# A two-layer adaLN network on one core: gates fixed with channels on partitions, the last pieces of layer 0 moved into the first attention steps, and one residual sum moved ahead

## Chip, cores and metric

The kernel runs on one core of one Trainium2 chip. The metric is the device time of one execution in microseconds (us), lower is better; the median of the runs counts. A profiled execution also gives a span (first to last instruction) and a time of its own.

## What is computed

Eight inputs (B = 8) of 512 rows by 128 channels pass through two adaLN layers. The reference, cut to what matters:

```python
mod = (silu(L0_c) @ L0_wmod)            # per input: sa, ca, ga, sb, cb, gb, 128 channels each
ga = (2 * (ga >= 0) - 1) * maximum(abs(ga), 0.25)      # the same for gb, and in layer 1
x = x + ga * rwkv_attention(layernorm(x) * (1 + ca) + sa)     # a scan over the 512 rows
x = x + gb * (fp6_quantised(layernorm(x) * (1 + cb) + sb) @ wd.T + bias)
# layer 1, with its own mod
h = layernorm(x) * (1 + ca) + sa
gate = softmax((h @ w_gate).mean(rows)) # 3 numbers per input
idx = sort(top_k(h @ w_imp, 32))        # 32 selected rows per input
out = gate0 * attn(q, latent keys) + gate1 * attn(q, selected keys) + gate2 * attn(q, window keys)
x = x + ga * (out @ w_proj)             # 16 heads of 96 channels, 32 value channels
h = layernorm(x) * (1 + cb) + sb
x = x + gb * tanh(h @ wo.T + c_final @ uo.T + bo)   # c_final: a cell that runs over the 8 inputs
```

## The kernel before

Everything stays in SBUF. The program is written out by hand for five engines, each with its own stream; semaphores join them. It has three parts.

**Setup.** TensorE makes all modulation columns in one PSUM bank (L1609); VectorE copies them to `modc` (L1151: channels on partitions, 12 kinds by 8 inputs). Four kinds are needed as rows as well (the same 128 values on all partitions), because they scale the columns of `woT` and of the dequantised weight or the rows of the second norm. For each input TensorE makes these four with a 128x512 product (L1616) and layer 1's output gates with a 128x128 product (L1617); ScalarE copies the first to `modrow` (`row_read`, L816), VectorE the second to `garow1` (`row_reads`, L1162). VectorE then fixes the gates (sign, at least 0.25; `gate_fix`, L1124 to L1129) on 128x1024 elements three times: for `modrow[:, :, 0]`, for `modrow[:, :, 3]` and later for `garow1`. `ffn_rows` (L1172, L1173) adds one to the scales and makes the bias row.

**Start: layer 0.** A loop over `b` from -2 to 9 is written out, a round per value. In round `b` the engines work at different inputs: moments of input `b+2` (`norm_mix`, VectorE), key maxima of `b+1` (`maxima`, L1202 and L1206), the scan `wkv` of `b` (L1212 to L1232), first residual sum of `b` with its moments (`norm_ffn`, L1237), quantisation of `b-1` (`quantised_ffn`, L1077 to L1089), second residual sum of `b-1` with its moments (`norm_attention`, L1247), and layer 1's norm and transposition into `HT` of `b-2`. VectorE's order within a round is: `wkv(b)`, `quantised_ffn(b-1)`, `maxima(b+1)`, `norm_ffn(b)`, `keep_moments(b-2)`, `norm_mix(b+2)`, `norm_attention(b-1)`. GpSimd turns moments into scale and shift (`deviation`), modulates (L656, L658), decodes the codes (`decode`, L651), rotates queries and keys (`rope`, L663 to L676). ScalarE normalises (L820) and makes the exponentials (L848 to L854) that `wkv` of the next round waits for. The first projections for layer 1's attention go through one shared PSUM bank, bank 7, in the order of the table `SLOTS`: TensorE fills it (`fill`), ScalarE or VectorE reads it (`read`), and the next fill waits for that read. The scores of rows (`score`, L1679) are summed in bank 5 in two halves of four inputs; the top 32 of the first half are found in round 6. After round 9 TensorE makes the gate logits (`gate_logits`, L1859).

**Attention: layer 1.** 32 groups of four heads, four groups per input. A group has 24 units (a unit is the score tiles of one head); `RU` = 12 units of the latent keys, then 12 of the window keys. `FIRST` is the first group, `FULL` a loop of four groups, seven times, and `LAST` the rest. `group_tasks` says at which unit which fill of bank 7 stands. SyncE moves rotated and projected parts into place by DMA (`lay_group`: 4 KB runs, four DMAs a part); TensorE waits for all of a group's parts in front of its unit 0. In `FIRST` VectorE also finds the top 32 of the second half of the inputs (units 0 to 12) and the softmax of the gates.

## Time and profile before

| | before |
|---|---|
| median of 3 runs | 2014.3 us (2013.28 to 2017.04) |
| the profiled execution's own time | 2014.44 us |
| its span | 2012.6 us |
| TensorE busy | 1822.4 us, 91% |
| VectorE busy | 1287.3 us, 64% |
| ScalarE busy | 1173.0 us, 58% |
| GpSimd busy | 677.5 us, 34% |
| mean granted TensorE clock | 0.947 |

Busy shares are averages over parts that differ: in the first seventh of the span VectorE is the busiest, behind it TensorE. They say where to look; what a part is worth is read from its timeline. In the timeline, a number in square brackets is the idle time of that engine just before the instruction, and the name behind the arrow is what ended it.

### The profile page before, as it was taken

The page shows a single profiled execution, that of the slowest core. Times are in us where ns is not written, and L with a number is a line of the kernel's source. Part 1 is how long each engine was busy: PE and PEld are TensorE (multiplying, and loading weights), DVE is VectorE, ACT ScalarE, POOL GpSimd, SP SyncE. Part 2 cuts the span into 40 slices and gives each one's busy share as a digit, 9 for nine tenths or more (in the row PEclk, how much of TensorE's full clock was granted, in tenths as well). Part 3 has the DMA queues.
Part 4 walks back from the last instruction along what each step waited for, and adds up shares of the span by engine and source line. Part 5 has one row for each costly group of instructions (what it writes and reads, how often), then busy time and mean ns, then how long its engine had stood idle before and what let it go on. Part 6 is the DMA issues. An engine that isn't in the chain of part 4 may idle for free.

```text
span 2012.6 us, 38380 instructions
## 1 busy us (share of the span) xinstructions
PE 1822.4 (91%) x10672; PEld 1076.1 (53%) x10672; DVE 1287.3 (64%) x3817; ACT 1173.0 (58%) x3572; POOL 677.5 (34%) x698
## 2 busy tenths in 40 slices
PE   5575789999999999999999999999999999999996
PEld 3332445555555555655555555555655556555552
DVE  6999666656566666666666656665666666666672
ACT  3464356656565656666565656665666566666651
POOL 1456433343233323333343333332333234333300
PEclk8778589999999999999999999999999999999998
DMA  4001021111011111121112111120111111211101
GB/s 157 1 0 27 15 58 38 38 43 52 24 40 39 47 35 38 42 48 48 39 38 52 48 26 47 35 54 20 44 43 38 49 38 38 52 48 38 37 1 42
DMA packets 71346, 81.42 MB, mean 40 GB/s; under 512 B 29521, under 2 KB 37842, under 8 KB 70994
## 3 DMA queue, kind: packets, MB, share of 16 engines
q1 hardware_dynamic: 71122, 78.74, 15.4%
q8 instruction: 103, 1.69, 0.4%
q14 instruction: 121, 0.99, 0.2%
HBM read 7.90 MB, written 2.10 MB: 5 GB/s over the span
## 4 chain that ended last, share of the span: by engine, by line
issue 49%; PE 21%; POOL 19%; DVE 8%; ACT 2%; POOLq 1%; DMA 0%; DVEq 0%; SPq 0%; ACTq 0%
PE bank L1822 6%; PE bank L1849 3%; POOL arena L674 3%; PE bank L1783 3%; POOL arena L676 3%; POOL arena L663 2%; POOL arena L673 2%; POOL arena L664 2%; PE bank L1688 2%; POOL arena L672 1%; POOL arena L712 1%; DVE arena L1225 1%; PE bank L1683 1%; PE bank L1746 1%; PE bank L1729 1%
## 5 line engine op out<-in xcount | busy, mean ns | idle before, releaser
L1425 DVE CUSTOM_DVE_ANT_0 arena<-bank,W 128x512 f32<-128x512 f32 (+3 forms) x1024 | 480.6, 488 | 523.0 <-PE bank L1822 363.9
L980 ACT ACTIVATE arena<-arena 128x512 f32<-128x512 f32 (+3 forms) x1024 | 570.4, 560 | 369.5 <-DVE arena L1425 366.6
L1822 PE MATMUL bank<-arena 96*128 96x512 f32 (+6 forms) x2048 | 716.5, 452 | 15.9 <-issue 14.5
L1822 PEld LDWEIGHTS bank<-arena 96*128 96x128 f32 x2048 | 350.2, 192 | 190.5 <-issue 154.5
L1849 PE MATMUL bank<-W,arena 128*128 128x128 f32 x2560 | 430.0, 282 | 0.1
L1849 PEld LDWEIGHTS bank<-W,arena 128*128 128x128 f32 x2560 | 301.4, 144 | 222.1 <-issue 183.3
L1436 DVE COPY arena<-bank 128x512 f32<-128x512 f32 (+1 forms) x512 | 318.5, 622 | 78.6 <-PE bank L1849 75.8
L712 POOL TENSOR_TENSOR arena<-arena,one 128x512 f32<-128x512 f32 x64 | 66.8, 1044 | 812.2 <-DVE arena L1393 806.2
L1783 PE MATMUL bank<-arena 128*32 128x256 f32 (+1 forms) x3072 | 223.2, 363 | 1.9 <-DVE arena L1436 1.8
L980 ACT ACTIVATION_READ_ACCUMULATOR arena<-arena 128x1 f32 x1024 | 197.3, 193 | 0.0
L959 ACT ACTIVATE arena<-bank 128x384 f32<-128x384 f32 x256 | 124.6, 487 | 94.4 <-PE bank L1849 92.6
L1783 PEld LDWEIGHTS bank<-arena 128*32 128x32 f32 x3072 | 61.0, 108 | 184.8 <-issue 158.9
L663 POOL TENSOR_TENSOR arena<-arena,W 128x512 f32<-128x512 f32 x64 | 69.9, 1092 | 205.4 <-ACT arena L898 205.4
L974 ACT ACTIVATE arena<-bank 128x32 f32<-128x32 f32 (+1 forms) x384 | 65.2, 205 | 105.0 <-DVE arena L1425 103.8
L1688 PE MATMUL bank<-arena,W 128*128 128x512 f32 x192 | 103.1, 619 | 21.9 <-ACT arena L898 21.8
L1687 PE MATMUL bank<-arena,LW 96*128 96x512 f32 x192 | 103.3, 620 | 2.8 <-ACT arena L898 2.7
L672 POOL TENSOR_TENSOR arena<-arena 128x512 f32<-128x512 f32 x64 | 81.4, 1272 | 56.1 <-DMA arena<-arena 50.0
L1623 PE MATMUL bank<-W,arena 128*128 128x128 f32 x160 | 34.0, 351 | 71.6 <-ACT arena L820 45.3
L898 ACT ACTIVATE arena<-bank 128x512 f32<-128x512 f32 x128 | 76.2, 595 | 33.4 <-PE bank L1687 19.4
L1425 DVE DVE_READ_ACCUMULATOR2_ANT arena<- 128x1 f32 x1024 | 84.8, 83 | 0.0
L676 POOL TENSOR_TENSOR arena<-arena 128x512 f32<-128x512 f32 x64 | 81.3, 1270 | 5.0
L674 POOL TENSOR_TENSOR arena<-arena,W 128x512 f32<-128x512 f32 x64 | 78.0, 1220 | 0.0
(265 smaller groups left out, 2221.0 us busy)
## 6 DMA issues: line engine op xcount, KB each, us to landing
arena<-arena SPq DMA_DIRECT2D x896, 64.0 KB, 2.0
arena<-arena SPq DMA_DIRECT2D x64, 128.0 KB, 2.6
W<-wide SPq DMA_DIRECT2D x1, 3730.0 KB, 13.4
X<-x SPq DMA_DIRECT2D x8, 256.0 KB, 5.5
out<-arena SPq DMA_DIRECT2D x8, 256.0 KB, 2.3
arena<-arena SPq DMA_DIRECT2D x96, 16.0 KB, 1.9
LW<-lat SPq DMA_DIRECT2D x1, 768.5 KB, 14.3
arena<-mods SPq DMA_DIRECT2D x1, 768.0 KB, 4.5
```

Source lines behind the costliest of these rows:

```text
L663: step(pool.tensor_tensor(rt[:, 2], rt[:, 0], w("cos"), ALU.mult))
L674: step(pool.tensor_tensor(rt[:, 1], rt[:, 1], w("cos"), ALU.mult))
L676: pool.tensor_tensor(stX2, rt[:, 0], rt[:, 1], ALU.add).then_inc(s_rope, 1)
L959: A(turned(turn, k), turned_bank(turn, k), ACT.Copy).then_inc(s_pa, 1)
L980: done = A(here, here, ACT.Exp, bias=nmax[:, c:c + 1], scale=-1.0, accum_out=lsum[:, c:c + 1])
L1425: last = v.tensor_tensor_reduce(Pb[:, s % 4, at_p:at_p + n], bank[turn.score_bank(s)][:, at + lo:at + lo + n], w("mask", T - n), -1.0, 3e3 ...
L1436: CP(turned(turn, k), turned_bank(turn, k)).then_inc(s_pd, 1)
L1687: return MM(dst[:], LW[0:QL, col:col + P], latT[0:QL], start=True, stop=True)
L1688: return MM(dst[:], w("wink", col, P), hTc, start=True, stop=True)
L1783: last = MM(bank[5][rows, low * 2 * P:low * 2 * P + n], V[a][turn.g(q) % 2][:, c, rows], PT[low][:, h, c * 2 * P:c * 2 * P + n], start=(c ...
L1822: last = MM(B_[:, at:at + lo + n], query(t), Kb[a][g % 2][0:QD, h, skip:skip + lo + n], start=True, stop=True)
L1849: last = pe.transpose(bank[3 + k % 2][:, n * P:(n + 1) * P], Pb[:, k % 4, c * P:(c + 1) * P], ident)
```

## The change

- `gate_fix` runs once, in setup, on the four gate kinds of `modc` (128x32 elements, channels on partitions). `brow`, the gated bias, is made there too, as a column. `row_reads`, `row_gates`, `ffn_rows`, L1616 and L1617 go away, and with them the DMA of the bias row.
- Rows are made when needed: TensorE multiplies a `modc` column, repeated over 128 columns, by the identity (`spread_rows`, 4 products of 128x128). `rows(b+1)` stands at the end of round `b` of TensorE, after `score`; ScalarE's `row_read(b)` in round `b` after `mix_input`; `modrow` has two buffers in place of eight. Layer 1's output gates come in two batches of four inputs (`output_gates`), read by ScalarE.
- `norm_attention(b-1)` stands in front of `norm_mix(b+2)` on VectorE.
- The start ends with round 8. The last input's norm, its transposition (`z3T`), the second half's `score`, the gate logits (`gates`) and the selected values (`vs`) become fills of bank 7 in `FIRST`, at units 2, 4, 7 and 12; the second top 32 moves from units 2 to 12 to units 6 to 16.
- `SLOTS` is set anew: the first top 32's rank, rows and keys stand one slot to one round earlier on TensorE; VectorE forms `tokens` in round 6, `pick` ahead of `wkv` in round 7 and reads `ks` behind it. GpSimd decodes input 7 before it rotates the first group's keys.
- The semaphore for rotated parts is split in queries (`s_lq`) and keys (`s_lx`); TensorE waits for window keys in front of unit 12, and SyncE lays window keys before latent ones.

```diff
-READER = {"op": "dve", "ks": "dve", "o2": "dve", "rank": "dve"}
+READER = {"op": "dve", "ks": "dve", "o2": "dve", "rank": "dve", "score": "dve", "gates": "dve"}
...
-        extra = [(14, "rank")] if first else [(12, "z4T"), (14, "gf"), (15, "gi"), (19, "gc")]
+        extra = [(2, "z3T"), (4, "score"), (7, "gates"), (12, "vs"), (17, "rank")] if first else [(12, "z4T"), (14, "gf"), (15, "gi"), (19, "gc")]
...
-         (6, "mid"): "vw", (6, "out"): "x1k", (6, "end"): "x2k",
-         (7, "mid"): "rank", (7, "out"): "nk3", (7, "end"): "sel",
-         (8, "top"): "ks", (8, "out"): "nk1", (8, "end"): "vl", (9, "out"): "vs"}
+         (6, "mid"): "vw", (6, "out"): "x1k", (6, "end"): "rank",
+         (7, "top"): "sel", (7, "next"): "ks", (7, "out"): "x2k", (7, "end"): "nk3",
+         (8, "top"): "nk1", (8, "mid"): "vl"}
...
@@ gpsimd, start @@
-            for b in range(-2, B + 2):
                 if 0 <= b < B:
-                    if b == 0:
-                        pool.wait_ge(s_rowg, 1)
+                    pool.wait_ge(s_rowsa, b + 1)
                     gate_wo(b)
                 if 0 <= b - 1 < B:
                     decode(b - 1)
+                if b == B:
+                    rope(start, "k", 0)
...
@@ scalar, start and attend @@
+                if 0 < b < B:
+                    row_read(b)
+                if 0 <= b < 2:
+                    output_gates(b)
...
+                    if turn.first and s == 1:
+                        normed_attention(B - 1)
...
@@ vector, setup @@
-            gate_fix(modc[:, 11], gmx, gsm)
-            step.settle()
-            TS(gsm, gmx, 1.0, None, ALU.mult).then_inc(s_setup, 1)
+            gate_fix(modc[:, 2:12:3], ta, tb)
+            step.settle()
+            step(TS(brow, modc[:, 5], vec("b0"), None, ALU.mult))
+            step.settle()
+            CP(cells[:, 1:2], cells[:, 0:1]).then_inc(s_setup, 1)
...
@@ vector, start @@
                 if 0 <= b - 2 < B:
                     keep_moments(b - 2)
+                if 0 <= b - 1 < B:
+                    norm_attention(b - 1)
                 if 0 <= b + 2 < B:
                     norm_mix(b + 2)
                 if b == -2:
                     quantise_weight()
-                    row_reads()
-                    v.wait_ge(s_rowsa, B)
-                if b == 0:
-                    row_gates(garow1[:])
-                    TS(gsm, gmx, 1.0, None, ALU.mult).then_inc(s_gproj, 1)
-                if 0 <= b - 1 < B:
-                    norm_attention(b - 1)
...
@@ tensor @@
+            def spread_rows(dst, columns):
+                for n, column in enumerate(columns):
+                    last = MM(dst[:, n * P:(n + 1) * P], column.to_broadcast([P, P]), ident, start=True, stop=True)
+                return last
+
+            def rows(b):
+                if b > 0:
+                    pe.wait_ge(s_var2, b)
+                spread_rows(bank[4], [modc[:, n, b:b + 1] for n in range(2, 6)]).then_inc(s_rows, 1)
...
-                if 0 <= b - 2 < B:
-                    score(b - 2)
+                if 0 <= b - 2 < HALF_B:
+                    score(bank[5], b - 2).then_inc(s_sc, 1)
+                if 0 <= b < B - 1:
+                    rows(b + 1)
...
-            gate_logits()
```

**VectorE, the end of round 0.** Before (L1237 first residual sum, `X` moments `norm_mix(2)`, then the output gates' `gate_fix`):

```order
L1237 TENSOR_TENSOR arena<-X,bank 128x512
L1056 BN_STATS small<-arena 128x6 x4
L1060 BN_AGGR small<-small 128x2 x4
L1056 BN_STATS small<-X 128x6 x4
L1060 BN_AGGR small<-small 128x2 x4
L1124 TENSOR_SCALAR arena<-garow 128x1024
L1125 SCALAR_TENSOR_TENSOR arena<-garow 128x1024
L1127 TENSOR_SCALAR arena<-arena 128x1024
L1129 SCALAR_TENSOR_TENSOR garow<-arena 128x1024
L1545 TENSOR_SCALAR small<-small 128x8
```

In the changed kernel (L1252 is the first residual sum, L1227 the start of `wkv(1)`):

```order
L1252 TENSOR_TENSOR arena<-X,bank 128x512
L1087 BN_STATS small<-arena 128x6 x4
L1091 BN_AGGR small<-small 128x2 x4
L1087 BN_STATS small<-X 128x6 x4
L1091 BN_AGGR small<-small 128x2 x4
L1227 SCALAR_TENSOR_TENSOR arena<-arena 128x512
```

The five instructions on `garow` are gone, and `wkv(1)` follows `norm_mix(2)` at once.

**VectorE, the end of round 1 in the changed kernel** (L1252 first sum, L1262 second sum, L1227 `wkv(2)`):

```order
L1252 TENSOR_TENSOR arena<-X,bank 128x512
L1087 BN_STATS small<-arena 128x6 x4
L1091 BN_AGGR small<-small 128x2 x4
L1262 TENSOR_TENSOR X<-arena,bank 128x512
L1087 BN_STATS small<-X 128x6 x4
L1091 BN_AGGR small<-small 128x2 x4
L1087 BN_STATS small<-X 128x6 x4
L1091 BN_AGGR small<-small 128x2 x4
L1227 SCALAR_TENSOR_TENSOR arena<-arena 128x512
```

Before, the pair of moments of the coming input stood between the first sum's moments and the second sum; now it stands behind the second sum and its moments.

**TensorE, the last rows ahead of the first attention scores.** Before (L1623 transpositions, first that of input 7's codes, L1661 bias, L1666 product of `ffn`, L1679 `score`, L1733 `vl`, L1725 `vs`, L1859 gate logits, L1822 attention scores):

```order
L1623 MATMUL bank<-W,arena 128x128 x4
L1661 MATMUL bank<-arena,ones_row 128x512
L1666 MATMUL bank<-arena 128x128 x4
L1679 MATMUL bank<-HT,impd 8x512
L1733 MATMUL bank<-LW,arena 128x128 x4
L1623 MATMUL bank<-W,arena 128x128 x4
L1725 MATMUL bank<-W,arena 32x128 x4
L1679 MATMUL bank<-HT,impd 8x512
L1859 MATMUL bank<-W,hsum 128x3 x8
L1822 MATMUL bank<-arena 128x512
L1687 MATMUL bank<-arena,LW 128x512
```

In the changed kernel (L1640 transpositions, first that of input 6's norm, L1756 `vl`, L1676 bias, L1681 product, L1846 attention scores, L1873 transposed probabilities):

```order
L1640 MATMUL bank<-W,arena 128x128 x4
L1756 MATMUL bank<-LW,arena 128x128 x4
L1640 MATMUL bank<-W,arena 128x128 x4
L1676 MATMUL bank<-W,arena 128x512
L1681 MATMUL bank<-arena 128x128 x4
L1846 MATMUL bank<-arena 128x512
L1700 MATMUL bank<-arena,LW 128x512
L1846 MATMUL bank<-arena 128x416
L1700 MATMUL bank<-arena,LW 128x512
L1846 MATMUL bank<-arena 128x512
L1873 MATMUL bank<-W,arena 128x128 x4
L1640 MATMUL bank<-W,arena 128x128 x4
```

The scores start right behind input 7's `ffn`; the transposition of input 7's norm (the last row) now stands behind unit 2. Behind unit 4 and unit 7 stand (L1692 `score`, L1730 gate logits, L1701 projections of window keys):

```order
L1700 MATMUL bank<-arena,LW 128x512
L1846 MATMUL bank<-arena 128x512
L1873 MATMUL bank<-W,arena 128x128 x4
L1692 MATMUL bank<-HT,impd 8x512 x4
L1846 MATMUL bank<-arena 128x416
```

and, three units later:

```order
L1846 MATMUL bank<-arena 128x416
L1873 MATMUL bank<-W,arena 128x128 x3
L1730 MATMUL bank<-W,hsum 128x3 x8
L1846 MATMUL bank<-arena 128x288
L1846 MATMUL bank<-arena 128x160
```

Four products of scores and eight of logits now stand between units of the first group.

## Rows read from the trace of the kernel before

**Rows 1.** Stretches: from:to, length, busy PE PEld DVE ACT POOL (instructions), TensorE clock, DMA share, GB/s
```profile
208.30:229.60 21.30, 12.18 (x35) 7.00 (x36) 18.41 (x39) 6.13 (x15) 9.27 (x13) 0.58 0.00 0
229.60:263.60 34.00, 26.79 (x95) 16.72 (x94) 9.91 (x35) 9.24 (x24) 15.97 (x22) 0.55 0.17 37
263.60:314.30 50.70, 47.70 (x268) 28.15 (x269) 39.73 (x116) 30.76 (x98) 15.36 (x13) 0.96 0.18 48
314.30:2000.00 1685.70, 1599.04 (x9868) 953.21 (x9866) 1033.32 (x3205) 1028.16 (x3241) 546.77 (x509) 0.98 0.16 40
```

**Rows 2.** Timeline, VectorE, first inputs: start us, us, engine, line, operation, out<-in, count [idle <-releaser]
```profile
13.01 0.17 DVE L1157 TENSOR_SCALAR small<-small 128x8 f32<-128x8 f32 x1
...
40.06 1.19 DVE L1212 TENSOR_TENSOR_SCAN arena<-arena 128x512 f32<-128x512 f32 x1
...
56.16 0.69 DVE L1237 TENSOR_TENSOR arena<-X,bank 128x512 f32<-128x512 f32 x1 [0.72 <-PE bank L1648]
...
59.25 0.66 DVE L1124 TENSOR_SCALAR arena<-garow 128x1024 f32<-128x1024 f32 x1
...
63.17 1.22 DVE L1212 TENSOR_TENSOR_SCAN arena<-arena 128x512 f32<-128x512 f32 x1
```

**Rows 3.** Timeline, other engines, first and second input
```profile
16.07 0.20 POOL L632 TENSOR_TENSOR small<-small 128x4 f32<-128x4 f32 x1
...
33.54 0.60 ACT L842 ACTIVATE arena<-bank 128x512 f32<-128x512 f32 x1 [5.51 <-PE bank L1640]
...
37.57 1.04 ACT L854 ACTIVATE arena<-arena 128x1024 f32<-128x1024 f32 x1
...
47.28 2.08 PE L1639 MATMUL bank<-arena,W 128*128 128x512 f32 x2 [0.87 <-ACT arena L836]
...
54.21 1.02 PE L1640 MATMUL bank<-arena 128*128 128x512 f32 x2
```

**Rows 4.** Timeline around the two sums of the fifth and sixth round
```profile
147.64 0.86 DVE L1056 BATCH_NORM_STATS2 small<-X 128x6 f32<-128x128 f32 x4
...
148.06 2.08 PE L1666 MATMUL bank<-arena 128*128 128x128 f32 x8
...
150.17 0.69 DVE L1247 TENSOR_TENSOR X<-arena,bank 128x512 f32<-128x512 f32 x1 [1.25 <-PE bank L1666]
...
152.10 1.19 DVE L1212 TENSOR_TENSOR_SCAN arena<-arena 128x512 f32<-128x512 f32 x1
...
169.55 1.16 PE L1666 MATMUL bank<-arena 128*128 128x128 f32 x8
...
171.73 0.65 DVE L1247 TENSOR_TENSOR X<-arena,bank 128x512 f32<-128x512 f32 x1
```

**Rows 5.** Timeline, last input up to the first scores
```profile
208.31 1.19 DVE L1212 TENSOR_TENSOR_SCAN arena<-arena 128x512 f32<-128x512 f32 x1
...
222.66 1.84 DVE L1293 TENSOR_SCALAR arena<-X,stat 128x128 f32<-128x128 f32 x4
...
225.01 0.67 DVE L1237 TENSOR_TENSOR arena<-X,bank 128x512 f32<-128x512 f32 x1
...
243.01 1.05 POOL L651 TENSOR_TENSOR arena<-arena,small 128x512 f32<-128x512 fp8e4 x1
...
249.27 0.69 DVE L1247 TENSOR_TENSOR X<-arena,bank 128x512 f32<-128x512 f32 x1 [6.31 <-PE bank L1666]
...
263.66 2.05 PE L1822 MATMUL bank<-arena 96*128 96x512 f32 x2 [1.39 <-ACT arena L943]
```

**Rows 6.** Timeline, TensorE: one product of scores, the gate logits
```profile
125.23 1.02 PE L1679 MATMUL bank<-HT,impd 128*8 128x512 f32 x2
...
258.70 3.58 PE L1859 MATMUL bank<-W,hsum 128*128 128x3 f32 x16
```

**Rows 7.** Timeline, last key transfers of a later group, its successor's first scores
```profile
455.56 1.51 SPq L542 DMA_DIRECT2D arena<-arena  x2
...
468.53 1.02 PE L1822 MATMUL bank<-arena 96*128 96x512 f32 x2
```

More of the change, by code:

```diff
@@ L326, in build @@
         xdT = cv(T)
-        z3 = cv(NT, P)
         q8 = cv(P).bitcast(FP8)
-        ta, tb = (Kb[1][0].rearrange("p h t -> p (h t)")[:, n * B * P:(n + 1) * B * P].rearrange("p (b c) -> p b c", b=B)
-                  for n in range(2))
+        ta, tb = cv(4, B), cv(4, B)
         cv = Carve()
@@ L684, in shared_key @@
                 if moved is not None:
[L685 removed]
+                    pool.wait_ge(s_lx, moved * (16 * 2 * HG))
                 pool.tensor_tensor(stX1[0:ROPE], rt[0:ROPE, 2], rt[0:ROPE, 3], ALU.add).then_inc(s_kr, 1)
@@ L922, in read @@
                     last = A(latT, G[:], ACT.Copy)
+                elif name == "z3T":
+                    last = A(HT[:, (B - 1) * T:], G[:], ACT.Identity, bias=modc[:, 6, B - 1:B],
+                             scale=modc[:, 7, B - 1:B], accum_out=hsum[:, B - 1:B])
+                    last.then_inc(s_ga, 1)
+                    act.wait_ge(s_ga, turn.read("z3T"))
+                    act.sem_inc(s_h3, 1)
+                    return
                 elif name == "vs":
@@ L951, in attend @@
                         read(turn, *task)
-                    if turn.first and s == 2:
+                    if turn.first and s == 1:
+                        normed_attention(B - 1)
+                    if turn.first and s == 9:
                         act.wait_ge(s_gs, 1)
@@ L1306, in read @@
                     v.wait_ge(s_gd, turn.read("o2", k))
+                elif name == "score":
+                    step(CP(top, G[0:B]))
+                    CP(marked, G[0:B]).then_inc(s_gd, 1)
+                    v.wait_ge(s_gd, turn.read("score"))
+                elif name == "gates":
+                    CP(gates[:].rearrange("p b n -> p (b n)"), G[:, 0:3 * B]).then_inc(s_gd, 1)
+                    v.wait_ge(s_gd, turn.read("gates"))
+                    gates_shifted()
                 elif name == "rank":
@@ L1499, in _ @@
             start = Turn(START)
-            for b in range(-2, B + 2):
-                if b == -1:
-                    row_gates(modrow[:, :, 0])
+            for b in range(-2, B + 1):
+                if b == 7:
+                    read(start, "rank", 0)
+                    for j in range(NT):
+                        last = pick(0, j)
+                    last.then_inc(s_zc, 1)
                 if 0 <= b < B:
                     wkv(b)
+                if b == 7:
+                    read(start, "ks", 0)
                 if b == 4:
@@ L1514, in _ @@
                     top_ranked()
+                    for j in range(NT):
+                        tokens(0, j)
                 if 0 <= b - 1 < B:
                     quantised_ffn(b - 1)
-                if b == 7:
-                    read(start, "rank", 0)
-                    for j in range(NT):
-                        tokens(0, j)
-                    for j in range(NT):
-                        last = pick(0, j)
-                    last.then_inc(s_zc, 1)
-                if b == 8:
-                    read(start, "ks", 0)
                 if 0 <= b + 1 < B:
                     maxima(b + 1)
-                if b == -1:
-                    row_gates(modrow[:, :, 3])
-                    ffn_rows()
                 if b == 0:
@@ L1707, in fill @@
                         last = pe.transpose(G[:, j * B:(j + 1) * B], top[:, j * P:(j + 1) * P], ident[0:B, 0:B])
+                elif name == "z3T":
+                    pe.wait_ge(s_z3, B)
+                    last = turn4(G, z3)
+                elif name == "score":
+                    for b in range(HALF_B, B):
+                        last = score(G, b)
+                elif name == "gates":
+                    pe.wait_ge(s_h3, B)
+                    for b in range(B):
+                        last = MM(G[:, 3 * b:3 * b + 3], hsum[:, b:b + 1].to_broadcast([P, P]), w("gate"), start=True, stop=True)
                 elif name == "sel":
@@ L1853, in attend @@
                         fill(turn, *task)
-            def gate_logits():
-                pe.wait_ge(s_h3, B)
-                pe.wait_ge(s_var3, B)
-                for b in range(B):
-                    last = MM(bank[6][:, 3 * b:3 * b + 3], hsum[:, b:b + 1].to_broadcast([P, P]), w("gate"), start=True, stop=True)
-                last.then_inc(s_gl, 1)
             start = Turn(START)
@@ L1867, in slot @@
                     fill(start, name, 0)
-            for b in range(-2, B + 2):
+            rows(0)
+            for b in range(-2, B + 1):
                 if b == 3:
@@ L1872, in _ @@
                 slot(b, "top")
+                slot(b, "next")
                 if 0 <= b + 1 < B:
```

205 lines of the change are left out of this document (97 added, 108 removed).

## Prediction

> **What bounds the kernel now.** I read the span by stretches first. From 263.6 us on, in the attention, TensorE is busy 47.70 of the first group's 50.70 us and 1599.04 of the 1685.70 us behind it [rows 1]. Nothing in the change takes work from that part, so it can only gain ahead of 263.6 us, and it can lose in the first group. Then the timeline of VectorE over the start: from round 0 to round 7 its instructions stand back to back and its waits are few, one of 0.72 us [rows 2] and one of 1.25 us [rows 4] among them; it is the bound there, and each of its instructions that goes away is time. Then the timeline of all engines behind 208 us: in the 34.00 us before the first attention scores VectorE is busy 9.91 and TensorE, at a clock of 0.55, 26.79 [rows 1]; the last input's chain sets the time there, with a wait of 6.31 us in front of its second sum at 249.27 [rows 5]. Times below are from the start of the span; "new" marks the changed kernel's.
>
> **Setup and input 0.** Now `wkv(0)` starts at 40.06, because VectorE copies eight gate rows and fixes two sets first, though ScalarE's last exponential ended at 38.61 and could have come earlier still [rows 2, 3]. New: setup's small operations end at 13.18 [rows 2], and one more of 0.2 makes 13.4. TensorE's first `rows` are eight passes over 128 columns, as the product at 148.06, 2.1 us [rows 4]; ScalarE's copy takes 0.6, so 16.2. GpSimd has the shift by 16.3 [rows 3]. Norm 1.65, four transpositions 1.1 and `mix_input` 0.8, with 0.1 to 0.2 between engines, give 20.1. The three projections took 47.28 to 55.23, about 7.8 us, when they began at the lower clock [rows 3]: new 27.9. ScalarE's stretch from tanh to last exponential is 33.54 to 38.61, 5.1 us [rows 3]: `wkv(0)` starts at 33.1, **-7.0 us**.
>
> **Round 0.** `wkv(0)` to `wkv(1)` is 23.1 us now [rows 2]. The fixing of the output gates, 59.25 to 63.17, is 3.9 of it, and the 0.72 us wait for `project_out` goes because the projections are far earlier against VectorE [rows 2]. New 18.5, so `wkv(1)` at 51.6, **-11.6 us** in sum.
>
> **Rounds 1 to 5, the moved sum.** In round 4 TensorE's `ffn` product runs from 148.06 to 150.14 and VectorE takes the sum at 150.17; the 1.2 us of the coming input's moments (from 147.64) lie inside that wait [rows 4]. With the sum first, VectorE waits out those 1.2 us and does the moments afterwards: +1.2. In round 5 the product takes 1.16 us, is done at 170.71, and the sum at 171.73 comes a microsecond later than it could [rows 4]: there the move costs 0.2. What the earlier sum releases is GpSimd's shift for layer 1, which stands behind `modulate_ffn` on GpSimd anyway, so it buys nothing. Of the five rounds I put two at 1.2 and three at 0.2: **+3.0 us**. Bounds: 0 if the exponentials end the wait in any case, 5 x 1.2 = +6.
>
> The added `rows(b+1)` is 1.05 to 2.1 us of TensorE per round, the larger as at 148.06 [rows 4]; it stands where TensorE next waits for ScalarE's norm, and the copy of 0.6 us stands on ScalarE before it waits for TensorE's projections. Both cost nothing; without that cover they would cost 2.7 us a round. The bias product has 128 weight rows in place of one and the same 512 columns: nothing.
>
> **Rounds 6 and 7.** `tokens` (1.84 us [rows 5]) and the reading of `rank` with `pick` (0.9) move ahead of `wkv(7)`; TensorE makes `rank` only behind `rows(7)`, about 0.7 us after VectorE is free. So `wkv(7)` starts at 208.31 - 11.6 + 3.0 + 1.8 + 1.6 = 203.1 new.
>
> **The tail.** From `wkv(7)` to the first sum of input 7 it is 16.7 us [rows 5]; the reading of `ks` comes in where 2.6 us of `tokens` and `pick` go out, the same. New 219.8. Input 6 then sets the pace: decode 1.05 [rows 5], transpositions 1.1, bias 2.1 and product 2.1 at the lower clock end at 226.3; sum and moments 228.3; GpSimd 1.7, ScalarE's two slot reads and the norm to 233.3; transposition and `attention_input` to 235.5. Then input 7's transposition, bias and product, 5.4 us: **first scores at 241, against 263.66** [rows 5]. Input 7's decode now waits for no key rotation, which held it until 243.01 although its codes were ready 7 us earlier [rows 5]. The selected keys' DMAs are issued before 230 and hidden. Together the start gives **-22.6 us**.
>
> **The first group.** It takes in four products of scores, each 1.02 us at the upper clock with 0.86 from one to the next, 3.5 us; eight logits, 3.58 us at the lower clock [rows 6], 2.0 at the upper; a transposition 0.5 and `vs` 0.4. That is 6.5 us on an engine busy 94% of the group [rows 1]. For waits, none of which this trace has, the bounds are 0 and 7 us (fills stand at units 0 to 7 one by one, and each waits until the one before is read; ScalarE has 1.65 us of norm more at unit 1; `rank` is filled one unit behind VectorE's last step of the top 32, where two lay between). I take 3.0, nearer to the 3.0 us of the 50.7 in which TensorE idles now [rows 1]. **+9.5 us.**
>
> **Later groups.** The same instructions. The last transfers of a group are issued by 457.1 and the next group starts at 468.53 [rows 7], so the new order of SyncE's queue is hidden with some 9 us to spare. Zero.
>
> **The sum** is -22.6 + 9.5 = -13.1 us. Against the profiled execution (2014.44, of which 1.8 lie around its span) it gives 2001.3; its own time is 0.1 from the median of 2014.3, so **2001.3 us** stands for the median too. A measurement of this kernel tells a difference from none from about 0.2%, 4 us.
>
> **Where the clock comes in.** [...] The same `ffn` product takes 2.08 us in round 4, after TensorE stood idle for longer, and 1.16 us in round 5 [rows 4]. My sum keeps the lower level in the tail and in two rounds.
>
> [...]
>
> **Rivals.** (1) *The clock stays up*, since `rows` fills part of TensorE's idle time. Then the two waits of 1.2 us go, and bias, product and transposition of inputs 6 and 7 take 2.3 us less each: -13.1 - 2.4 - 4.6 = -20, 1994 us. For it: round 5 is already fast. Against: `rows` ends, and TensorE still idles some 3 us before the next norm comes. Chance 0.13. (2) *The first group pays more*: the serial fills stall TensorE by 7 us and two more come from the crowded ScalarE; -22.6 + 15.5 = -7, 2007 us. For it: VectorE too is busy 39.73 of 50.70 there [rows 1], and the top 32 now meets its work on the selected scores at units 13 to 16. Chance 0.14. (3) *The gain is given back*: ScalarE, an in-order queue, gets a copy more per round, its exponentials for the next input end late, and each of five rounds loses 2 us rather than 0.6 while the first group costs 12: -22.6 + 7 + 12 = -3.6, no change, 2011. Against: its copy stands before a wait. Chance 0.09. (4) *Slower*: the wait for latent keys stays in front of unit 0, and these parts are now the last in SyncE's queue, behind four window parts. If they came late in every group, each of 31 groups would start late; 0.9 us each is 28 us, less 13 makes +15, 2029 us. It decides from a landing 9 us later than now [rows 7]. Against: the queue's content is the same. Chance 0.04. My forecast keeps 0.60.
>
> **Numbers.** Faster 0.60 + 0.13 + 0.14 = 0.87, same 0.09, slower 0.04. The range, 1993.5 to 2008, takes in rivals 1 and 2 and the bounds of the terms (loop 0 to 6, waits of the first group 0 to 7) and leaves out rivals 3 and 4 and some of the ends.
>
> **What would show it.** Right: `wkv(0)` near 33 and `wkv(1)` near 52 us; no 128x1024 instruction on VectorE; waits of over 2 us for the `ffn` product before the second sum in rounds at the lower clock; first scores near 241; a first group of some 60 us; later groups of unchanged length. Wrong: `wkv(0)` past 36 us, the first scores past 246, or a first group above 64 us would each take the result out of the forecast; so would the steady groups, if any grew by 0.2 us.

## The result and the profile after

The changed kernel is slower: 2037.9 us in the median (2031.6 to 2045.8, 4 runs) beside 2015.7 for the kernel before on the same chip (2013.3 to 2020.2, 4 runs). The ratio is 1.0116, 95% interval 1.0075 to 1.0157, so about 23 us slower. The forecast was 2001.3, in a range of 1993.5 to 2008.0, with a chance of 0.04 for slower. It was wrong in sign. Its profiled execution took 2041.61 us, its span 2039.5.

The start did what was foreseen, and a little more. These are the changed kernel's rows that answer to [rows 1], [rows 2] and [rows 5]: the stretches, VectorE's scans of the first two inputs, and TensorE in the tail.

```profile
203.10:237.70 34.60, 22.23 (x89) 16.07 (x89) 21.73 (x52) 10.62 (x24) 23.28 (x27) 0.62 0.07 14
237.70:263.60 25.90, 22.73 (x78) 11.72 (x78) 12.60 (x38) 12.47 (x34) 13.18 (x17) 0.90 0.25 67
263.60:314.30 50.70, 47.47 (x289) 28.76 (x288) 34.28 (x105) 28.38 (x91) 10.84 (x10) 0.91 0.12 29
314.30:2030.00 1715.70, 1612.55 (x9815) 959.89 (x9814) 1038.07 (x3193) 1022.33 (x3225) 588.50 (x505) 0.97 0.16 39
```

```profile
32.70 1.23 DVE L1227 TENSOR_TENSOR_SCAN arena<-arena 128x512 f32<-128x512 f32 x1 [5.40 <-ACT arena L877]
...
50.94 1.19 DVE L1227 TENSOR_TENSOR_SCAN arena<-arena 128x512 f32<-128x512 f32 x1
```

```profile
234.23 1.92 PE L1676 MATMUL bank<-W,arena 128*128 128x512 f32 x2
235.94 1.91 PE L1681 MATMUL bank<-arena 128*128 128x128 f32 x8
237.65 1.63 PE L1846 MATMUL bank<-arena 96*128 96x512 f32 x2
...
243.86 1.13 PE L1700 MATMUL bank<-arena,LW 96*128 96x512 f32 x2 [3.03 <-ACT arena L921]
...
251.57 3.60 PE L1692 MATMUL bank<-HT,impd 128*8 128x512 f32 x8
```

The first scores come at 237.65 instead of 263.66, 26.0 us earlier. To see where that went I followed one instruction through all 32 groups, VectorE's step at unit 13 (line 1366 before, 1388 after). It comes 15.1 us earlier than before in the first group (278.91 against 294.05), 9.8 in the second (333.76 against 343.55), and from there each input loses about 5 us; in the last group it is 25.0 us late. So about 35 us were lost in the steady part, which my sum had put at zero. Two kinds of rows had changed there. GpSimd first: its operations on 128x512 in the groups (320 us to the end of the attention), the kernel before and then the changed one. Columns: line, operation, shapes, count, busy us, mean ns, idle before.

```profile
L676 POOL TENSOR_TENSOR arena<-arena 128x512 f32<-128x512 f32 x60 | 76.2, 1270 | 4.7
L674 POOL TENSOR_TENSOR arena<-arena,W 128x512 f32<-128x512 f32 x60 | 72.7, 1212 | 0.0
L664 POOL TENSOR_TENSOR arena<-arena,W 128x512 f32<-128x512 f32 x60 | 65.6, 1093 | 0.0
```

```profile
L693 POOL TENSOR_TENSOR arena<-arena,W 128x512 f32<-128x512 f32 x59 | 81.9, 1388 | 0.0
L680 POOL TENSOR_TENSOR arena<-arena,W 128x512 f32<-128x512 f32 x59 | 75.3, 1277 | 0.0
L695 POOL TENSOR_TENSOR arena<-arena 128x512 f32<-128x512 f32 x59 | 74.8, 1269 | 4.6
```

The multiplies of `rope` that read `cos` or `sin` in W take 0.18 us longer (1093 to 1277 ns); the addition, which reads only the arena, is as it was. TensorE's waits in the groups, before and then after (total us, times, longest):

```profile
PE bank L1688 <- ACT arena L898: 20.8, 30, 1.1
```

```profile
PE bank L1701 <- ACT arena L921: 30.2, 29, 1.7
...
PE bank L1806 <- issue: 2.1, 3, 1.1
```

TensorE waits 9.4 us more for ScalarE's copy of rotated parts, which stands behind `rope`. And at three places there is a pause without a releaser inside the value products (L1806) that the kernel before does not have at all.

### The profile page after: what moved, and what is told of

Read it like the earlier page. It is cut to its first block, busy times and chain, and to the rows that moved or that the text cites. A ratio compares the mean times of both kernels' runs of the same rounds, so it can differ in the third digit from the quotient of the medians.

```text
span 2039.5 us, 38502 instructions
## 1 busy us (share of the span) xinstructions
PE 1834.5 (90%) x10720; PEld 1091.7 (54%) x10720; DVE 1283.0 (63%) x3786; ACT 1174.2 (58%) x3574; POOL 730.1 (36%) x698
## 4 chain that ended last, share of the span: by engine, by line
issue 48%; PE 20%; POOL 18%; DVE 1%; ACT 1%; POOLq 1%; DVEq 0%; ACTq 0%
PE bank L1846 6%; PE bank L1873 3%; POOL arena L693 3%; POOL arena L692 3%; POOL arena L680 3%; PE bank L1806 3%; POOL arena L695 2%; POOL arena L679 2%; PE bank L1701 2%; POOL arena L731 1%; POOL arena L691 1%; PE bank L1696 1%; PE bank L1769 1%; PE bank L1752 1%; POOL arena L717 1%
## 5 line engine op out<-in xcount | busy, mean ns | idle before, releaser
L1846 PE MATMUL bank<-arena 96*128 96x512 f32 (+6 forms) x2048 | 728.2, 458 | 15.6 <-issue 15.6
L1846 PEld LDWEIGHTS bank<-arena 96*128 96x128 f32 x2048 | 356.9, 195 | 192.9 <-issue 155.9
L1873 PE MATMUL bank<-W,arena 128*128 128x128 f32 x2560 | 433.5, 283 | 0.1
L1873 PEld LDWEIGHTS bank<-W,arena 128*128 128x128 f32 x2560 | 303.6, 145 | 225.3 <-issue 186.0
L1806 PE MATMUL bank<-arena 128*32 128x256 f32 (+1 forms) x3072 | 229.1, 366 | 3.4 <-issue 2.1
L1806 PEld LDWEIGHTS bank<-arena 128*32 128x32 f32 x3072 | 62.4, 109 | 192.0 <-issue 167.4
L679 POOL TENSOR_TENSOR arena<-arena,W 128x512 f32<-128x512 f32 x64 | 81.6, 1275 | 196.2 <-ACT arena L921 196.2
L1701 PE MATMUL bank<-arena,W 128*128 128x512 f32 x192 | 102.8, 618 | 32.1 <-ACT arena L921 31.9
L1640 PE MATMUL bank<-W,arena 128*128 128x128 f32 x160 | 34.5, 355 | 63.4 <-ACT arena L843 41.0
L693 POOL TENSOR_TENSOR arena<-arena,W 128x512 f32<-128x512 f32 x64 | 88.7, 1385 | 0.0
```

What stands on the lines that cost most here:

```text
L679: step(pool.tensor_tensor(rt[:, 2], rt[:, 0], w("cos"), ALU.mult))
L693: step(pool.tensor_tensor(rt[:, 1], rt[:, 1], w("cos"), ALU.mult))
L1701: return MM(dst[:], w("wink", col, P), hTc, start=True, stop=True)
L1806: last = MM(bank[5][rows, low * 2 * P:low * 2 * P + n], V[a][turn.g(q) % 2][:, c, rows], PT[low][:, h, c * 2 * P:c * 2 * P + n], start=(c ...
L1846: last = MM(B_[:, at:at + lo + n], query(t), Kb[a][g % 2][0:QD, h, skip:skip + lo + n], start=True, stop=True)
L1873: last = pe.transpose(bank[3 + k % 2][:, n * P:(n + 1) * P], Pb[:, k % 4, c * P:(c + 1) * P], ident)
```

## Experiments

A run whose name begins with a_ or after_ stands on the changed kernel, one with b_ on the kernel before, and mb is a measurement of single operations. **Theory A** is that one column more in `vecs` shifts every later column of W, and that cos and sin at their new place make GpSimd slower. **Theory B**, my rival 4, is that the new order of SyncE's transfers costs the groups. **Theory C** is that the earlier start lets the groups meet the clock in another way.

### Padding the columns

```diff
-        ("vecs", 10),
+        ("vecs", 11),                     # b_pad11; 12 in b_pad12 and, on the changed kernel, in a_pad12
-        ("cos", T), ("sin", T),
+        ("gap", 1), ("cos", T), ("sin", T),                # b_tab, with vecs at 10
```

*a_pad12* (the changed kernel, vecs 12): 

> The changed kernel with one zero column added behind b0, so that every later column of the weight tile (ident, the weights, cos, sin, mask) lies again at an even fp32 column, two columns further than in the kernel before. Theory A (odd columns: GpSimd's multiplies that read cos and sin are slower there): these multiplies fall from 1.27 us back to 1.09, GpSimd's busy time from 730 us to about 678, the wait of TensorE for ScalarE's copy of the rotated keys falls back to under 1.2 us in each group, and the time is 1998 to 2008 us. Theory B (the new order of SyncE's transfers and TensorE's later wait for the keys cost the groups): the steady groups stay as they are, 2030 to 2040 us. Theory C (TensorE's slow spells come from where the start moved the groups, whatever the columns): GpSimd falls to 678 us, but the time only to 2020 to 2032.

*b_pad11*: 

> The kernel before with one unused zero column behind its ten, nothing else. Theory A: cos and sin at odd columns, their multiplies 1.27 us, GpSimd's busy time about 730 us, TensorE waits longer for the rotated keys, and the kernel is 20 to 40 us slower, 2035 to 2055. Theory B: no difference, 2012 to 2020, since the order is that of before. Theory C: GpSimd's operations slower, but the time 2015 to 2025.

*b_tab*: 

> The kernel before with the zero column placed directly ahead of cos: cos, sin, mask and iota move to odd columns, ident and all weights stay. If the rotations on GpSimd alone carry the loss, the time is that of the kernel with the column behind the ten (2035 to 2055), and so is GpSimd's busy time. If TensorE's reads of ident and the weights, or ScalarE's, carry it, the time is 2012 to 2020 although GpSimd is at 730 us.

*b_pad12*: 

> The kernel before with two unused zero columns: everything later moved by 8 bytes, an even column again. Theory A: as before, 2012 to 2020 us, GpSimd 677 us. If any shift costs (alignment to 16 or 32 bytes, or size), it is slower by some 20 us too.

Measured against the kernel before, 2012.6 us: b_pad11 2042.6, ratio 1.017 (1.0146 to 1.0193); b_tab 2044.0, 1.0149 (1.0132 to 1.0165); b_pad12 2041.5, 1.0156 (1.0135 to 1.0176); a_pad12 2030.3, 1.009 (1.0076 to 1.0105). One unused column ahead of cos, and nothing else, costs the kernel before 31 us, more than the whole change. B and C fall as the only causes, since neither order nor start differ in b_tab. But A was wrong in its rule: two columns are as bad as one. The row of b_tab, then TensorE's wait in it:

```profile
L664 POOL TENSOR_TENSOR arena<-arena,W 128x512 f32<-128x512 f32 x60 | 76.7, 1278 | 0.0
```

```profile
PE bank L1688 <- ACT arena L898: 32.7, 30, 1.8
```

From unit 13 of the first group to that of the last, b_tab takes 29.1 us more than the kernel before (1674.4 against 1645.4). Longer waits of TensorE for the rotated parts are 11.9 of it. Another 7.2 are waits ahead of the transposition of the normed attention output (7.5 us in 5 waits against 0.3 in one):

```profile
PE bank L1623 <- DVE arena L1334: 7.5, 5, 1.6
```

VectorE's line 1334 waits in its turn for `rstd`, which GpSimd makes. The last 10.1 are the same products taking longer (1584.8 us busy against 1574.8), at a granted clock of 0.98 against 0.99. a_pad12 is the changed kernel with cos 0 bytes into a 16-byte unit and not 12, and is about as slow as the changed kernel (1.009 and 1.0116, with intervals that overlap).

### Which place is fast

```diff
+            for n in range(32):
+                pool.tensor_tensor(flat[:, 0:T], W[:, 1064:1064 + T], W[:, 3008 + n:3008 + n + T], ALU.mult).then_inc(s_mb, 1)
+                pool.wait_ge(s_mb, n + 1)
```

*mb*: 

> The kernel before with 64 GpSimd multiplies of 128x512 put ahead of GpSimd's first work, each of two slices of the weight tile into the arena, one after the other: 32 with the first operand fixed and the second moved on by one fp32 column each, 16 of the same with the first operand 8 columns earlier, 16 with both operands fixed (24 bytes apart modulo 64, as the table and the rotated parts are in the kernel before) and the output moved on by a column each. The time of the whole is of no interest. If what matters is where the two operands lie to each other within 64 bytes, the first 32 show 1.09 us at a repeating set of columns (period 16) and 1.27 at the others, and the set moves with the first operand in the next 16. If it is the second operand's own address, the set stays. If only 32 bytes matter, the period is 8. If the output matters, the last 16 differ among themselves.

The trace has 1.26, 1.09, 1.09, 1.26 us for n = 0 to 3, and repeats this with period 4 through all 32. The next 16, with the first operand 8 columns earlier, show the same at the same n, and the last 16, with only the output moved, are all 1.09. So the second operand's place in a unit of 16 bytes, counted from the start of the tile W, decides: 4 or 8 bytes into it is fast, 0 or 12 slow. (Of the first operand only two places, both multiples of 16 bytes, were tried, and the output was moved only with the second operand at a fast place.) cos began at column 6686, 8 bytes into a unit; the change moved it to 6687, 12 bytes in; with one column more than that it is at 0, as in b_pad12 and a_pad12. All three fit.

```diff
-        ("cos", T), ("sin", T),
+        ("gap", 15), ("cos", T), ("sin", T),               # a_gap15; ("gap", 16) in b_gap16
```

*a_gap15*: 

> The changed kernel with 15 unused columns placed directly ahead of cos, so that cos, sin, mask and iota lie 16 columns (64 bytes) further than in the kernel before, and at its place within 64 bytes. Theory A in its new form (the place of cos and sin within 64 bytes decides GpSimd's speed, and that alone carries the loss of the steady groups, as the kernel before with a gap ahead of cos lost 31 us): GpSimd's busy time 678 us, the multiplies 1.09, and 1998 to 2008 us. Rival (the new order of transfers and the clock carry part of it): GpSimd at 678 us but the time 2012 to 2030.

*b_gap16*: 

> The kernel before with 16 unused columns ahead of cos. New form of theory A: 64 bytes are a full period, so nothing changes: 2009 to 2017 us, GpSimd 677 us. If it is not the place within 64 bytes but the distance to the arena, the 128-byte line or the tile's size: slower, 2035 to 2048.

b_gap16 took 2012.2, ratio 1.0008 (0.9999 to 1.0018): a wider tile costs nothing. a_gap15 took 2017.9 beside 2010.1, 1.0031 (1.0018 to 1.0045), with the multiplies back at 1092 ns. About 17 of the 23 us are cos and sin. The rival in the expectation holds too: something more is lost, since the start still brings its 16.6 us by unit 13 of the first group, and it is gone at the end. It goes at the loop heads. First the kernel before, then a_gap15, TensorE at the head of the loop over the inputs; then the stretches between unit 13 on either side of a head, before and a_gap15:

```profile
526.18 1.43 PE L1822 MATMUL bank<-arena 96*128 96x512 f32 x2 [2.19 <-issue]
527.54 1.08 PE L1783 MATMUL bank<-arena 128*32 128x256 f32 x8
```

```profile
514.26 1.12 PE L1846 MATMUL bank<-arena 96*128 96x512 f32 x2 [2.58 <-issue]
515.31 0.63 PE L1806 MATMUL bank<-arena 128*32 128x256 f32 x1
517.00 1.08 PE L1806 MATMUL bank<-arena 128*32 128x256 f32 x7 [1.05 <-issue]
```

```profile
509.20:568.30 59.10, 54.63 (x326) 32.14 (x325) 34.90 (x105) 34.01 (x105) 16.11 (x14) 0.97 0.14 33
```

```profile
496.90:560.40 63.50, 57.66 (x326) 33.09 (x324) 34.86 (x105) 33.93 (x104) 16.10 (x14) 0.92 0.13 31
```

Each jump back costs a pause without a releaser, 2.0 to 2.9 us (once 3.6), in every kernel. In a_gap15 a second one, 0.4 to 1.5 us, follows about two microseconds later at 5 of 6 heads. The stretch shown is 4.4 us longer: TensorE is idle 1.4 us more and busy 3.0 us more with the same products, at a granted clock of 0.92 against 0.97. **Theory D**: the second pause comes from where the loop begins in TensorE's code. In the compiled program that is instruction 1649 before and 1738 after, since the start has more products.

### The loop's place in the code

```diff
+            for _ in range(78):                     # a_pc39, on a_gap15; two waits make one instruction
+                pe.wait_ge(s_set, 1)
             pe.wait_ge(s_silu, 1)
```

*a_pc39*: 

> The changed kernel with the gap of 15 columns ahead of cos, and 39 more instructions of TensorE (waits on a semaphore long passed, before its first work), so that the loop over the inputs begins at the same place in TensorE's code, counted modulo 128 instructions, as in the kernel before. Theory D (the loop's place in the code makes the second pause after each loop head, up to 1.5 us in the value products right behind the head, and with it the longer spell at the low clock): these pauses are gone, the stretch from unit 13 of the last group to unit 13 of the next input's first one takes 59 to 61 us as before instead of 61.3 to 64, and the time is 1998 to 2008 us. Theory E (the phase in which the earlier start lets the groups meet the clock, or chance): 2012 to 2022 as without them. Theory B (order of transfers): the same, 2012 to 2022.

*b_pc89* (178 waits, on the kernel before): 

> The kernel before with 89 more waiting instructions at TensorE's start, so that its loop begins at exactly the place in TensorE's code at which that of the changed kernel begins (instruction 1738). Theory D: pauses of 0.4 to 1.5 us in the value products (L1785) right behind the loop head, and 6 to 20 us slower, 2016 to 2032. Theories B and E: no difference, 2008 to 2015 us.

*a_oldq*: 

> The kernel a_pc39 with SyncE's order in the groups behind the first put back to that of before (window keys laid only after the latent keys are read) and TensorE's wait for the window keys put back to unit 0. Theory B (that order costs or saves something): over 4 us faster or slower than a_pc39. Theories D and E: within 2 us of a_pc39, since SyncE and the keys are well ahead of the units in the steady groups.

a_pc39 took 2005.0 beside 2011.5, ratio 0.9969 (0.9955 to 0.9983). The second pauses are gone, and from the third group to the last the step at unit 13 is 11 to 13 us earlier than before, without drift. b_pc89 took 2033.1, 1.0116 (1.0091 to 1.0142), with a second pause at five of six heads, 1.8 us in all:

```profile
PE bank L1785 <- issue: 1.8, 5, 0.5
```

Its six stretches around the heads take 373.8 us together against 359.0 before. Its first product, though, came at 11.08 instead of 6.42 us, because 89 waiting instructions (its page counts 38469 instructions against 38380) outlast TensorE's idle time; in its profile 2.5 us are lost by the first group and 12 behind it. a_oldq took 2009.0, 0.9991 (0.9977 to 1.0005), 4 us more than a_pc39 where theories D and E had foreseen at most 2; the intervals just overlap. In its profile, a run above its median, 3.2 us are lost by unit 13 of the first group, 4.6 by the second, and from there on it drifts by 5 us more. The old order of transfers is at any rate not better, so theory B, that the new order costs the groups, falls.

The page's row for the queue that carries instructions (packets, MB, share) goes with it. Before, changed, a_pc39:

```profile
q8 instruction: 103, 1.69, 0.4%
```

```profile
q8 instruction: 110, 1.80, 0.4%
```

```profile
q8 instruction: 104, 1.70, 0.4%
```

The four kernels whose loop begins at 1738 (the changed one, a_pad12, a_gap15, b_pc89) fetch 109 or 110 packets, all others 103 or 104: six more, and there are six jumps back.

*after_pc39* (the changed kernel with the 78 waits alone): 

> The changed kernel as it was, with TensorE's 39 additional waits alone (its loop at the place modulo 128 of the kernel before, its tables at their odd place). Theory D with A, adding up: the place in the code gives back 10 to 16 us, the tables' 17 to 25 stay lost: 2020 to 2030. If the place matters only together with the tables' place, 2003 to 2012 or still 2035.

*a_pc103* (206 waits): 

> As a_pc39, but with 103 instead of 39 more instructions ahead of TensorE's loop (64 more: its head is at instruction 1841, which is that of the kernel before modulo 64, not modulo 128). If 64 is a full period of the effect: 2001 to 2009 us and no second pause. If not: it can be anything up to a_gap15 (2010 to 2022).

*a_pc23* (46 waits): 

> As a_pc39, but with 23 more instructions (head at instruction 1761: that of the kernel before modulo 16, not modulo 32 or 64). If 16 is a full period: 2001 to 2009. If the distance to a boundary of 64 or more decides: between a_pc39 and a_gap15 or worse, 2005 to 2022, with pauses behind the loop head.

The last two test **theory F**: the bad starts are a whole range, in which each of the six jumps back fetches one packet more and TensorE stands behind it, and 1689 lies in that range and 1657 does not. Of b_pc40 it wanted 109 packets, a first product at the old 6.4 us and 2018 to 2032 us; of b_pc8 103 packets and 2009 to 2015 us. Where the range ends rested on a number of instructions in a packet that I took for granted and that no run shows.

*b_pc40* (80 waits, on the kernel before; the loop at 1689): 

> The kernel before with 40 more waiting instructions at TensorE's start (80 waits, two to an instruction), which fit into its idle time before the first product; its loop head moves from instruction 1649 to 1689. The instruction queue's row counts 103 packets of 16.4 KB in the kernel before, 109 to 110 in the three kinds whose loop begins at 1738, 104 in those at 1761, 1777 and 1841. [...] Rival (the loss of the kernel with 89 more came from its later start, 11.1 against 6.4 us, and chance): 103 packets, 2009 to 2015 us.

*b_pc8* (16 waits, on the kernel before; the loop at 1657): 

> [...] Rival (any added instruction or any move of the loop costs): slower by 3 us or more, or more packets.

after_pc39 took 2020.4, ratio 1.0035 (1.0023 to 1.0046): 16 us of the loss come back by the place in the code alone, and about 17 came back by the tables alone. Together they gave 30 (from 1.0116 to 0.9969), so the two causes nearly add up: either is worth 16 to 17 us undone alone, and 12 to 13 undone second. In the kernel before the same displacement of the tables cost 31 us; in after_pc39 the waits for the rotated parts are longer too (31.8 against 20.6 us in a_pc39), but there are none ahead of the transposition. a_pc23 took 2005.4, 0.9951 (0.9934 to 0.9968). a_pc103 took 2011.9, 0.999 (0.9977 to 1.0002), but its first product came at 12.59 us against 7.12 in a_pc39, and the stretches around its loop heads are as short as there (59.2 to 59.6 us). Neither has a second pause. b_pc40, with its loop at 1689, took 2013.3, 1.0015 (1.0005 to 1.0025), and 104 packets, no second pause. b_pc8 took 2010.8, 0.9999 (0.9988 to 1.0009), 103 packets.

So **theory F** falls as I had put it: 1689 should have been a bad start, and b_pc40, with its first product at 6.88 us, has neither the packets nor the loss. What fits all seven starts (1649, 1657, 1689, 1738, 1761, 1777, 1841) is narrower. In the traces of the four kernels that begin at 1738 all 16 second pauses stand at the same place, 12 or 13 instructions behind the loop's start, which is instruction 1750 or 1751. If one packet ended there and the next began, a loop from 1738 would get some 12 instructions from the packet it jumps into and then stand for the next; one at 1689 would get about 60, in which the next could arrive, and those at 1761 and 1777 would lie behind the edge. That is my account of the pauses and not a test of it: no run moved the start step by step towards the edge, and no trace shows which instructions a packet holds. What the pages show is packets of 16.4 KB (1.69 MB by 103): 103 with the loop at 1649 or 1657, 104 at 1689, 1761, 1777 or 1841, and 109 or 110 at 1738. Why six more come at 1738 alone is not settled, nor how near to the edge is too near.

How much of the loss is the pause itself? The six stretches around the heads take 374.4 us together in a_gap15 and 357.4 in a_pc39, and the second pauses are 5.0 of the 17 us. a_pad12 has three of them, 1.5 us in all, and its stretches still take 371.3, against 361.1 in after_pc39, whose tables are slow as well. The greater part is TensorE's products at the lower clock. That the place of the loop costs it is shown by a_pc39 and after_pc39, which moved nothing else; that the second pause is what brings the lower clock is read from their order in time and was not tested apart.

### The moved sum, and what else the rule gives

```diff
                 if 0 <= b + 2 < B:
                     norm_mix(b + 2)
                 if 0 <= b - 1 < B:
                     norm_attention(b - 1)        # a_nm: as before, behind norm_mix
```

```diff
-        rt = cv(4, T)
+        rtf = cv(4 * T + 8)                      # a_rt
+        rt = [rtf[:, at:at + T] for at in (0, T + 1, 2 * T + 4, 3 * T + 5)]
```

*a_nm*: 

> The kernel a_pc39 with the second residual sum put back behind the coming input's moments in VectorE's rounds, as in the kernel before. The prediction charged this move with +3.0 us (within 0 and +8). If so, 1999 to 2005 us, and the first scores of the attention up to 3 us earlier than at 237 us. If the sum in front hastens the tail instead, first scores later and 2005 to 2010.

*a_rt*: 

> The kernel a_pc39 with the second and fourth of the four tiles of the rotation moved on by one fp32 column, so that the subtraction and the addition too have a second operand 4 bytes past a multiple of 16; cos and sin stay 8 bytes past one. Theory A, carried further (the second operand's place within 16 bytes is the price, here still paid by two of six operations): GpSimd's subtraction and addition fall from 1.27 to 1.09 us, each rotation is 0.36 us shorter, TensorE's waits for the rotated parts (20.6 us, 30 times) fall by up to 0.36 x 30 = 10.8 us, and the time is 1990 to 2000 us. If the first operand's place (rt 1 now 4 bytes past) costs in its turn, the multiplies grow and the time stays at 2003 to 2008 or gets worse.

*a_best*: 

> Both gains together: a_rt (second operand of all six operations of the rotation off the multiple of 16 bytes) and a_nm (the residual sum back behind the coming input's moments). If they add, as parts in different stretches should (5 to 6 us each against a_pc39): 1990 to 1997 us, the fastest of all. If one takes what the other gives: 1998 to 2001.

All three stand on a_pc39. a_nm took 2000.3, ratio 0.9942 (0.993 to 0.9955): the moved sum costs 5.4 us by the two ratios. VectorE's wait for the `ffn` product in a_pc39 and in a_nm:

```profile
DVE X L1262 <- PE bank L1683: 11.9, 6, 6.8
```

```profile
DVE X L1262 <- PE bank L1683: 9.7, 3, 6.7
```

Six waits instead of three, and from `wkv(2)` to `wkv(6)` each round is 0.6 to 2.0 us longer. But the waits grew by 2.2 us only. From `wkv(0)` to `wkv(7)` a_pc39 takes 169.4 us and a_nm 164.3; of these 5.1 us VectorE is idle 2.0 more and busy 3.1 more with the same instructions. Two of them in `wkv(3)`, a_pc39 and then a_nm:

```profile
100.27 1.64 DVE L1234 TENSOR_TENSOR arena<-arena 128x512 f32<-128x512 f32 x1
101.94 1.64 DVE L1237 TENSOR_TENSOR arena<-arena 128x512 f32<-128x512 f32 x1
```

```profile
101.59 0.71 DVE L1234 TENSOR_TENSOR arena<-arena 128x512 f32<-128x512 f32 x1
102.33 0.69 DVE L1237 TENSOR_TENSOR arena<-arena 128x512 f32<-128x512 f32 x1
```

In a_pc39 GpSimd's two operations of `modulate_ffn` run from 99.72 to 103.03, beside these two. In a_nm they run from 97.59 to 101.00, beside the scan L1231 and L1232, which then take 1.68 and 1.69 us instead of 1.22 and 0.66. The moved sum shifts GpSimd's work against VectorE's, and in five rounds it now meets the pair that loses more.

a_rt took 1998.8, 0.994 (0.9928 to 0.9952). Its subtraction fell from 1271 to 1094 ns, as foreseen, but TensorE's wait for rotated parts only from 20.6 to 19.6 us. The gain came later, in the stretch from unit 13 of an input's third group to that of its fourth, which shrank from 56.1 to about 55 us in three of the first seven inputs, and in six of them in a_best; how the shorter rotation gets there I did not trace. a_best, both together, took 1993.4 beside 2013.0, ratio 0.9895 (0.9877 to 0.9914): about 1% faster than the kernel before, and the two gains add up.

## Why the prediction was wrong

**Setup, round 0, the tail: right, in part by luck.** `wkv(0)` stands at 32.70 (forecast 33.1), `wkv(1)` at 50.94 (51.6), `wkv(7)` at 202.40 (203.1), and the first scores at 237.65 (241). The bias and the product of the last input took 1.92 and 1.91 us, at the lower clock as I had kept it (0.62 in the stretch up to 237.70); the gain is 26.0 instead of 22.6 us. That `wkv(7)` comes out so near is two errors that cancel: from `wkv(1)` to `wkv(6)` the changed kernel takes 4.1 us more than the kernel before (114.63 against 110.54) and not 3.0, and from there to `wkv(7)` 2.2 more (36.83 against 34.60) and not 3.4.

**The moved sum: right in sign, too small, and a term was missing.** +3.0 stood in the sum with 6 as bound (not 8, as the expectation for a_nm has it); a_nm shows 5.4. The waits for the `ffn` product, which were all that "two at 1.2 and three at 0.2" counted, are 1.8 us in the five rounds of a_pc39 and none in a_nm. What failed is that nothing stood for VectorE's own instructions: 3.1 us go to their running longer beside GpSimd's.

**The first group: too small.** The sum had +9.5. In a_pc39, where nothing else disturbs, the start is 26.9 us ahead at the first scores and 12.8 at unit 13 of the second group, so the group and its successor's beginning cost 14.1. These are the kernel before and a_pc39 from the first scores to unit 13:

```profile
263.66:294.05 30.39, 28.37 (x132) 15.31 (x132) 24.99 (x70) 17.63 (x59) 15.33 (x13) 0.94 0.19 53
```

```profile
236.78:278.19 41.41, 37.13 (x178) 19.46 (x176) 24.64 (x79) 21.18 (x70) 17.91 (x22) 0.92 0.28 71
```

TensorE is busy 8.8 us longer and idle 2.3 us longer there. The added pieces take 7.0 of it (score products 3.6, logits 1.9, transposition 1.1, `vs` 0.4), against 6.5 in the sum. One wait of 3.6 us comes ahead of the second group's keys, for the slot that ScalarE reads behind its norm, and one of 2.9 us behind unit 13, for the ranks. Some waits of the kernel before are gone, so up to unit 13 of the second group TensorE is idle 4.2 us more: more than the 3.0 I took and less than the bound of 7. The other 9.9 of the 14.1 are busy time, where the sum had 6.5. What the sum did not have at all is the clock: the same scores and transposed probabilities run 1.4 us longer at 0.92 than at 0.94, and the next stretch has 0.97 instead of 1.00. With 14.1 for 9.5 it came near to rival 2 (15.5).

**Later groups, "the same instructions. Zero.": this step failed.** The instructions were the same, but not their addresses. The step looked at what TensorE does and at SyncE's queue, and never at where operands and code lie. `("vecs", 11)`, the column for `b0` from which `brow` is made, is the first change of the whole diff, ahead of the lines picked out under "The change". It cost about 17 us through cos and sin, and the 89 more TensorE instructions ahead of the loop about 16 through the loop's place. Rival 4 had the sign and the form (a small loss in each of 31 groups) and the wrong mechanism: the new order of transfers costs nothing that a_oldq could give back.

With both undone the kernel is 0.31% faster than before, some 6 us in the median and 9.4 in the profiled execution, against a forecast of 13.1. Against the latter: the start was 4.3 better (26.9 for 22.6, the dearer sum already in it), the first group 4.6 worse, and 2.9 us more went behind unit 13 of the last group. There TensorE is busy 2.9 us longer (52.7 against 49.8) at a granted clock of 0.83 against 0.88, and idle as long as before (23.4). The median shows only half of the forecast gain.

## What to carry to other kernels

Ahead of the promise that a steady loop keeps its time, look at what the edit does to the columns of a packed tile and to the length of the code in front of the loop: a pad of one column cost 31 us here, more than the change was about, while 16 unused columns (b_gap16) or 16 idle waits (b_pc8) showed no cost. If operations of the same shape have two durations (1.09 and 1.27 us), find out what parts them before the edit; and compare the instruction queue's packets of the two kernels. Where a kernel comes out otherwise than its own steps say, follow one recurring instruction through both traces: the drift names the stretch.

## What the runs showed of the hardware

GpSimd's fp32 multiply of 128x512 took 1.09 us in mb with its second operand 4 or 8 bytes into a 16-byte unit of its tensor and 1.26 with it at 0 or 12. In the kernels the subtraction and addition of `rope` took 1.27 us with it at 0 (lines 672 and 676 of the kernel before) and 1.09 to 1.11 at 4 (a_rt), where the multiplies whose first operand had moved to 4 stayed at 1.09 to 1.10. One multiply of `rope` (L674) takes 0.12 us more than the others at either place, 1.21 and 1.39 us, which I did not trace. VectorE's fp32 product of 128x512 took 0.69 to 0.71 us, and 1.64 beside GpSimd's `modulate_ffn`. A jump back on TensorE cost 2.0 to 2.9 us here, once 3.6, and up to 1.5 us more with the loop's beginning 12 instructions ahead of the place at which the second pause falls; what the lower clock takes comes on top, 59.1 us becoming 61 to 64 for the same work. A chain of waits on a semaphore long passed is not free either: 89 such instructions put TensorE's first product at 11.08 us (b_pc89) and 103 at 12.59 (a_pc103), about 0.11 us for each of the 14 more.
